# A three-layer transformer block on one core: softmax maxima and residual of the second attention moved to TensorE, and four steps reordered

## The reference, cut to what matters

```
x = x + attn_a(layernorm(x))     # 16 heads of 64, causal, over the 256 tokens of a batch
x = x + ffn(layernorm(x))        # routed slots
x = x + attn_b(layernorm(x))     # below
x = x + ffn(layernorm(x))

def attn_b(x, Wq, Wk, Wv, Wo, bo):            # N=16 batches, S=256 tokens, D=128
    q = (x @ Wq.T).reshape(N, S, 16, 8).transpose(0, 2, 1, 3)      # k and v likewise
    att = einsum('nqhd,nkhd->nhqk', q, k)                          # q, k: head; h: token
    att = softmax(att / sqrt(8), axis=3)
    out = einsum('nhqk,nkhd->nqhd', att, v).reshape(N, S, D)
    return out @ Wo.T + bo
```

## Time and profile before

| what | value |
|---|---|
| three runs | 996.13, 1005.44, 1005.65 us (median 1005.44) |
| the profiled execution's own time | 997.58 us |
| its span in the profile | 995.8 us |
| PE busy | 814.4 us, 82% |
| PEld busy | 619.3 us, 62% |
| DVE busy | 698.0 us, 70% |
| ACT busy | 462.7 us, 46% |
| POOL busy | 409.1 us, 41% |
| TensorE's granted clock, mean | 0.914 |

### The profile page before, as it was taken

One profiled execution on the slowest core, in us unless ns is written; L12 is line 12 of the kernel. 1 busy time (PEld: TensorE's weight loads), 2 busy tenths in 40 slices (PEclk: granted clock), 3 DMA queues, 4 the chain that ended last, 5 costly groups with the idle time before them and its releaser, 6 DMA issues.

```text
span 995.8 us, 25347 instructions
## 1 busy us (share of the span) xinstructions
PE 814.4 (82%) x10180; PEld 619.3 (62%) x10180; DVE 698.0 (70%) x1589; ACT 462.7 (46%) x785; POOL 409.1 (41%) x302
## 2 busy tenths in 40 slices
PE   2999999999999999999958766678777877829655
PEld 1688788887888888888845535345455445415435
DVE  4666666667666676666675775478989898867764
ACT  1667666667666676667632321222233233204220
POOL 1445444544444454444431000056767767751000
PEclk9999999999999999999988787778999999957776
DMA  6000000000000000000000000001111111110002
GB/s 258 2 3 1 0 0 0 0 0 0 0 0 0 0 0 0 0 0 0 2 1 1 1 1 1 1 3 19 21 11 21 21 14 18 22 21 1 1 1 84
DMA packets 71585, 13.16 MB, mean 13 GB/s; under 512 B 66432, under 2 KB 70528, under 8 KB 70912
## 3 DMA queue, kind: packets, MB, share of 16 engines
q1 hardware_dynamic: 71552, 12.71, 5.9%
HBM read 8.51 MB, written 4.19 MB: 13 GB/s over the span
## 4 chain that ended last, share of the span: by engine, by line
PE 56%; DVE 19%; issue 10%; ACT 10%; POOL 3%; DMA 1%; DVEq 0%; ACTq 0%; SPq 0%; POOLq 0%
PE PS L519 6%; PE PS L476 4%; PE PS L335 4%; PE PS L692 3%; PE PS L412 3%; DVE b_prod L776 3%; PE PS L337 3%; PE PS L483 3%; PE PS L336 3%; ACT a_ph L545 3%; PE PS L512 2%; PE PS L683 2%; PE PS L957 2%; PE PS L455 2%; POOL b_w L833 2%
## 5 line engine op out<-in xcount | busy, mean ns | idle before, releaser
L620 POOL TENSOR_TENSOR a_pl<-a_p,a_ph 128x1024 f16<-128x1024 f32 (+1 forms) x128 | 210.4, 1643 | 270.6 <-ACT a_ph L545 270.6
L542 ACT ACTIVATE a_p<-PS 128x1024 f32<-128x1024 f32 (+1 forms) x128 | 103.8, 811 | 89.1 <-PE PS L483 89.1
L833 POOL TENSOR_TENSOR b_w<-b_v,b_e 128x2048 f32<-128x2048 f32 x32 | 136.9, 4301 | 0.0
L587 DVE TENSOR_REDUCE a_nm<-PS 128x4 bf16<-128x512 f32 (+1 forms) x128 | 121.1, 946 | 0.4 <-PE PS L455 0.4
L576 DVE TENSOR_TENSOR a_qk_l<-PS,a_qk_h 128x512 f16<-128x512 f32 x128 | 87.9, 687 | 46.7 <-ACT a_qk_h L535 46.6
L545 ACT ACTIVATE a_ph<-PS 128x1024 f16<-128x1024 f32 (+1 forms) x128 | 102.9, 804 | 0.0
L535 ACT ACTIVATE a_qk_h<-PS 128x512 f16<-128x512 f32 x128 | 72.2, 604 | 58.0 <-PE PS L337 57.9
L683 PE MATMUL PS<-b_kh,w_rolls 128*128 128x256 f16 x256 | 68.7, 296 | 30.9 <-DVE b_prod L776 29.8
L776 DVE TENSOR_TENSOR b_prod<-PS,b_qt 128x512 f32<-128x512 f32 x128 | 84.1, 678 | 13.9 <-PE PS L685 13.7
L358 POOL TENSOR_TENSOR veps<-mv,eps 128x2 f32<-128x2 f32 (+2 forms) x40 | 7.9, 197 | 190.3 <-DVE mv L1107 139.1
L583 DVE TENSOR_TENSOR a_vl<-PS,a_vh 128x512 f16<-128x512 f32 x64 | 44.3, 692 | 54.8 <-ACT a_vh L538 54.8
(11 more groups left out here) (212 smaller groups left out, 2069.9 us busy)
## 6 DMA issues: line engine op xcount, KB each, us to landing
scratch_dram<-b_o SPq DMA_DIRECT2D x32, 64.0 KB, 4.0
b_y<-scratch_dram SPq DMA_DIRECT2D x16, 128.0 KB, 2.0
out_dram<-X SPq DMA_DIRECT2D x2, 1024.0 KB, 3.9
w_rest<-rest_dram SPq DMA_DIRECT2D x1, 1846.0 KB, 15.1
X<-x_dram SPq DMA_DIRECT2D x1, 1792.0 KB, 11.2
w_first<-first_dram SPq DMA_DIRECT2D x1, 1600.0 KB, 6.8
w_rolls<-rolls_dram SPq DMA_DIRECT2D x1, 512.0 KB, 15.3
X<-x_dram SPq DMA_DIRECT2D x1, 256.0 KB, 3.3
```

What stands on the lines that cost most here:

```text
L542: act.activation((a_p0, a_p1)[j][:, me, :, :, :].rearrange("p a h q -> p a (h q)"), TT[:, :, 0:512 - 256 * j], ACT.Exp, scale=EA ** -0.5)
L587: dve.tensor_reduce(a_nm[:, nx, j, :].rearrange("p (a h) -> p a h", a=2)[:, :, 0:2], MM[:, :, 0:256 * (j + 1)].rearrange("p a (h k) -> p a ...
L620: pool.tensor_tensor(*(n[:, g % 2, :, :, :].rearrange("p a h q -> p (a h q)") for n in (pl, p, ph)), ALU.subtract).then_inc(a_split, 1)
L833: pool.tensor_tensor(b_w8[:, j, :, :, :], rolled_values(par, j, 0, H), rolled_exps(par, j, 0, H), ALU.mult).then_inc(b_weighed, 1)
```

## The change

Eight things are changed.

- First attention: in each group `lo 0` comes behind `maxrow`; in group 2 `xt` comes behind `exps 1` and `exph 1`.
- Second attention, maxima: VectorE reduces them negated and rounded to bf16 (`b_nm`); a new step `shift` adds them on TensorE to the scores in the bank, by a product with the bf16 identity, and ScalarE takes the exponential straight from the bank. `flip` no longer starts the bank afresh with each product but with its first alone. `v` and the matmuls of roll 0 (`early`) are ahead of `soft`.
- Residual and bias: `project` first adds the bias in two f16 halves for both tiles at once, then `X` by a product with the identity, then Wo. `add` is now a copy by ScalarE.
- `normal` comes between `weigh 0` and `weigh 1`.
- `roll 7` comes ahead of `xt`.
- `qk`: ScalarE copies K first, then waits for K's low half, then copies Q and raises a new semaphore `b_q`, for which roll 0 on VectorE and the next fill of the bank wait.
- The last statistics wait for the added batches, since another engine writes them.
- Three small VectorE instructions are added to the constants.

```diff
@@ -74,8 +74,9 @@
             steps.extend((kind, g, n) for kind, n in new if cond)
-        put(prepare, ("qk", 0), ("qk", 1), ("lo", 0))
+        put(prepare, ("qk", 0), ("qk", 1))
         put(True, ("maxrow", 0))
+        put(prepare, ("lo", 0))
         put(not (first and g < 2), ("normal", 0))
...
         put(g == 2 and not last, ("apply", 0))
@@ -87,11 +88,11 @@
         put(g == 1 and not last, ("norm", 0))
-        put(g == 2 and not last, ("xt", 0))
         put(prepare, ("masks", 1))
...
         put(True, ("exps", 1), ("exph", 1))
+        put(g == 2 and not last, ("xt", 0))
         put(g == 1 and not first, ("project", 0))
...
         put(last and g == 3, ("ffn_apply", 0))
@@ -107,22 +108,26 @@
             steps.extend((n[0], par, n[1]) if isinstance(n, tuple) else (n, par, 0) for n in names)
+    put(one, "v", "early")
     put(True, "soft")
     put(two, "norm")
-    put(one, "v", ("roll", 0), ("roll", 1))
+    put(True, "shift")
+    put(one, ("roll", 0), ("roll", 1))
     put(before, "yt")
-    put(former, ("gather", 1), "normal")
+    put(former, ("gather", 1))
     put(two, "apply")
-    put(True, ("weigh", 0), ("weigh", 1))
+    put(True, ("weigh", 0))
+    put(former, "normal")
+    put(True, ("weigh", 1))
     put(one, ("roll", 2))
...
     put(before, "add")
-    put(one, ("roll", 6), ("flip", 0))
+    put(one, ("roll", 6), ("flip", 0), ("roll", 7))
     put(two, "xt")
-    put(one, ("roll", 7), ("dots", 1))
+    put(one, ("dots", 1))
     put(True, ("gather", 0))
...
     put(one, ("flip", 1))
@@ -133,7 +138,7 @@
               ("project", 1, 0)]
-B_PROLOGUE = [("norm", 0, 0), ("apply", 0, 0), ("xt", 0, 0), ("qk", 0, 0), ("v", 1, 0)]
+B_PROLOGUE = [("norm", 0, 0), ("apply", 0, 0), ("xt", 0, 0), ("qk", 0, 0), ("v", 1, 0), ("early", 1, 0)]
 for m in range(ROLLS):
...
 B_PROLOGUE += [("flip", 1, 0), ("flip", 1, 1), ("norm", 1, 0), ("apply", 1, 0), ("xt", 1, 0), ("qk", 1, 0)]
@@ -242,7 +247,8 @@
         ident, identb = w["ident"], w["identb"]
-        ones = sb("ones", [128, 128])
+        ones, ones_h = sb("ones", [128, 128]), sb("ones_h", [1, 128], F16)
+        b_bo_h, b_bo_l = sb("b_bo_h", [1, D], F16), sb("b_bo_l", [1, D], F16)
         a_wqk_h, a_wqk_l = sb("a_wqk_h", [128, 8, 2, 128], F16), sb("a_wqk_l", [128, 8, 2, 128], F16)
...
         b_w_h, b_w_l = sb("b_w_h", [128, 3, 128], F16), sb("b_w_l", [128, 3, 128], F16)
@@ -312,7 +318,7 @@
         b_e = sb("b_e", [128, 2, QT, H, H])
-        b_m, b_rs = sb("b_m", [128, QT, H]), sb("b_rs", [128, 2, QT, H])
+        b_nm, b_rs = sb("b_nm", [128, QT, H], BF16), sb("b_rs", [128, 2, QT, H])
         b_w8 = sb("b_w8", [128, QT, H, EB, H])
...
         b_o = sb("b_o", [128, QT, H, EB])
@@ -625,9 +631,10 @@
         b_stats, b_rstd, b_normed = sem("b_stats"), sem("b_rstd"), sem("b_normed")
+        b_q = sem("b_q")
         b_xh, b_xl, b_hi, b_lo, b_values = sem("b_xh"), sem("b_xl"), sem("b_hi"), sem("b_lo"), sem("b_values")
         b_rolled, b_multiplied, b_dotted = sem("b_rolled"), sem("b_multiplied"), sem("b_dotted")
-        b_shifted, b_exped, b_weighed, b_normal = sem("b_shifted"), sem("b_exped"), sem("b_weighed"), sem("b_normal")
+        b_maxed, b_shifted, b_exped, b_weighed, b_normal = sem("b_maxed"), sem("b_shifted"), sem("b_exped"), sem("b_weighed"), sem("b_normal")
         b_raised, b_flipped = sem("b_raised"), sem("b_flipped")
...
         b_stored, b_loaded, b_turned, b_added = sem("b_stored"), sem("b_loaded"), sem("b_turned"), sem("b_added")
@@ -645,7 +652,7 @@
             b = 2 * i + par
-            return {"qk": (b_lo, b + 3), "v": (b_values, b + 2), "yt": (b_turned, b - 1), "project": (b_added, b - 1),
+            return {"qk": (b_q, b + 3), "v": (b_values, b + 2), "yt": (b_turned, b - 1), "project": (b_added, b - 1),
                     "xt": (b_xl, b + 3)}[kind]
...
         def b_tensor(pe):
@@ -674,7 +681,12 @@
                     ins.then_inc(b_filled, 1)
-                elif kind == "roll":
+                elif kind == "shift":
+                    pe.wait_ge(b_maxed, b + 1)
+                    pe.matmul(O[par][:, :].rearrange("p (t s h) -> p t s h", t=QT, s=H), identb[:, :],
+                              b_nm[:, :, :].unsqueeze(2).to_broadcast([128, QT, H, H]), start=False, stop=True,
+                              skip_group_check=True).then_inc(b_shifted, 1)
+                elif kind == "early" or kind == "roll" and j > 0:
                     m = ROLLS * (b + 1) + j
...
                         pe.wait_ge(b_lo, b + 2)
@@ -695,14 +707,14 @@
                     if j == 0:
-                        wait(pe, b_shifted, b)
+                        wait(pe, b_exped, b)
                     for t in range(QT):
...
                                             ident[:, :].rearrange("p (n h) -> p n h", n=4)[:, :, 0:H],
-                                            start=True, stop=True)
+                                            start=j == 0 and t == 0 and e == 0, stop=False, skip_group_check=True)
                     ins.then_inc(b_flipped, 1)
...
                     pe.wait_ge(b_loaded, 16 * (b - 1))
@@ -711,14 +723,24 @@
                     pe.wait_ge(b_turned, b - 1)
+                    for bo in (b_bo_h, b_bo_l):
+                        pe.matmul(dst[:, 0:SEQ].rearrange("p (t d) -> p t d", t=QT), ones_h[:, :],
+                                  bo[:, :].unsqueeze(1).to_broadcast([1, QT, D]), start=bo is b_bo_h, stop=False,
+                                  skip_group_check=True)
                     for t in range(QT):
                         out_t = dst[:, t * 128:(t + 1) * 128]
-                        pe.matmul(out_t, b_yt[:, t * 128:(t + 1) * 128], w["b_wo"][:, :], start=True, stop=False)
-                        ins = pe.matmul(out_t, ones[0:1, :], w["b_bo"][:, :], start=False, stop=True)
+                        pe.matmul(out_t, ident[:, :], X[:, one_tile((b - 2) * QT + t), :].rearrange("p a d -> p (a d)"),
+                                  start=False, stop=False, skip_group_check=True)
+                    for t in range(QT):
+                        out_t = dst[:, t * 128:(t + 1) * 128]
+                        ins = pe.matmul(out_t, b_yt[:, t * 128:(t + 1) * 128], w["b_wo"][:, :], start=False,
+                                        stop=t == QT - 1, skip_group_check=True)
                     ins.then_inc(b_filled, 1)
...
         def b_scalar(act):
+            bank = [None]
+
             def do(step, i, fill):
...
                 b = 2 * i + par
@@ -728,8 +750,9 @@
                 elif kind == "qk":
-                    act.activation(b_qt[:, par, :], src[:, 0:SEQ], ACT.Copy)
                     act.activation(b_kh[:, par, :], src[:, SEQ:2 * SEQ], ACT.Copy).then_inc(b_hi, 1)
+                    act.wait_ge(b_lo, b + 3)
+                    act.activation(b_qt[:, par, :], src[:, 0:SEQ], ACT.Copy).then_inc(b_q, 1)
                 elif kind == "apply":
...
                     for t in range(QT):
@@ -745,20 +768,30 @@
                     act.activation(b_st[:, j, :], M[j][:, :], ACT.Copy).then_inc(b_raised, 1)
-                elif kind == "soft":
+                elif kind == "shift":
                     act.wait_ge(b_shifted, b + 1)
-                    act.activation(b_e[:, par, :, :, :], b_e[:, par, :, :, :], ACT.Exp, scale=EB ** -0.5).then_inc(b_exped, 1)
+                    act.activation(b_e[:, par, :, :, :], O[par][:, :].rearrange("p (t s h) -> p t h s", t=QT, s=H),
+                                   ACT.Exp, scale=EB ** -0.5).then_inc(b_exped, 1)
+                elif kind == "project":
+                    bank[0] = R[fill.bank], fill.count
+                elif kind == "add":
+                    projected, count = bank[0]
+                    act.wait_ge(b_filled, count)
+                    act.activation(X[:, bass.ds((b - 2) * QT, QT), :], projected[:, 0:SEQ]
+                                   .rearrange("p (t d) -> p t d", t=QT), ACT.Copy).then_inc(b_added, 1)
                 elif kind == "yt":
...
         def b_vector(dve, chain):
-            link, bank = chain.link, [None]
+            link = chain.link
 
...
                 if kind in ("ffn_stats", "ffn_apply"):
+                    if kind == "ffn_stats":
+                        dve.wait_ge(b_added, NB // 2)
                     early_norm(dve, link, kind, 1)
...
                     norm_stats(dve, link, X, (b + 2) * QT, QT).then_inc(b_stats, 1)
@@ -771,6 +804,8 @@
                     dve.wait_ge(b_rolled, ROLLS * (b + 1) + j + 1)
+                    if j == 0:
+                        dve.wait_ge(b_q, b + 2)
                     if j % 4 == 0:
...
                     dve.tensor_tensor(b_prod[:, j, :, :], T[j % 2][:, :].rearrange("p (e t) -> p e t", e=2),
@@ -779,9 +814,7 @@
                     sc = O[par][:, :].rearrange("p (t s h) -> p t h s", t=QT, s=H)
-                    link(dve.tensor_reduce(b_m[:, :, :], sc, X_AXIS, ALU.max))
```

(16 more changed lines are left out.)

## The result

The changed kernel takes 973.52 us (median of four runs, 972.47 to 975.52), the one before 1001.64 on the same footing (four runs, 996.13 to 1005.65): a ratio of 0.9725, 95% interval [0.9664, 0.9787]. The forecast was 980 from 1001, a ratio of 0.979. The kernel before runs at one of two levels: of 27 later executions 25 took 995.3 to 998.7 us and two about 1005, so the two at 1005 among the four here raise its median, and 23 to 25 us is a fairer size of the gain than 28. The profiled execution of the changed kernel took 972.47 us with a span of 970.7.

A forecast was written before the change was run, and what follows sets the result against it. TensorE was taken to bound the first attention, VectorE to pace the second. The terms, −2.0 − 17.5 − 1.2 − 0.6 + 0.4 = −20.9 us, taken off 1001, gave 980; range 966 to 998.

The forecast's parts named there:

- (a): First attention, `lo 0` behind `maxrow`: TensorE's gaps ahead of the maxima's product go, 0.65 us a batch, 10.4 us off.
- (b): First attention, `xt` behind `exph 1` in group 2: 0.89 us wait becomes about 1.7 elsewhere, costing 0.56 a batch, 8.4 us.
- (c): Second attention, maxima added on TensorE: VectorE loses the subtraction, 0.72 us a batch off the path.
- (d): Second attention, residual add moved to TensorE: frees 0.33 us of VectorE, costs TensorE 0.25 us a batch.
- (e): Second attention, roll 7 ahead of `xt`: 0.45 us less a batch, the chain then being roll 7, dots, projection, flip.
- (f): Second attention, `weigh 0` ahead of `normal`: hidden in steady state, 1.6 us off the last batch, 1.2 us net.
- (g): Second attention, `qk` copies K before Q: 0.6 us off in the two prologue batches, hidden in steady state.
- Rival 1: Second attention: the DRAM round trip is late, TensorE stands at `yt`, 0.5 to 0.6 us a batch back: 989; chance 0.12.
- Rival 3: First attention: the turning's new wait is covered, 8.4 us on become 13 off: 959; chance 0.04.
- Rival 4: Second attention: something unseen, such as TensorE's order, sets the pace and VectorE's freed time is idle: 999; chance 0.06.
- Rival 2: First attention gives nothing: the maxima's gap moves to the next wait, the turning costs 8.4 us: 990; chance 0.10.
- Rival 5: First attention: the turning's new 1.7 us wait lets TensorE's clock fall, 2 us lost a batch: 1010; chance 0.06.

The follow-up runs named there:

- experiment 3: Changed kernel with both edits of the first attention undone (`lo 0` ahead of `maxrow`, turning at its old place): 971.59 us, batch 30.55 us.
- experiment 1: Changed kernel with the turning of the next input (`xt`) in the first attention back at its old place: 962.45 us, batch 30.07 us.
- experiment 7: Changed kernel with the residual added by VectorE again, the bias still in two f16 products: 975.2 us.
- experiments 5 and 10: Changed kernel with roll 7 behind the turning again: 982.98 us; changed kernel with roll 7 and the turning both ahead of flip 0: 971.87 us.
- experiment 8: Changed kernel with maxima and their subtraction on VectorE again, `v` and roll 0 behind `soft`: 986.25 us.
- experiment 9: Kernel before the change with six unread f16 products more per batch of the second attention (batches 2 to 13): 993.32 us against 997.33.

## Why the prediction was right, point by point

The direction and the size were right: 20.9 us off the profiled run were forecast, 25.1 measured, 2.4 of which lie in a stage that the change doesn't touch. That the size came out so near is in part luck: the first attention missed by 6.0 us to the one side, and the clock, which the sum did not have, gave about 6 to the other.

- **(a) `lo 0` behind `maxrow`: half right.** All gaps ahead of the maxima's product closed, but the term was 0.65 us a batch and the edit is worth 0.48 (experiment 3 against 1). The step that failed is that `v` was the only consumer looked at. `pv` waits for the division, which is next in VectorE's order, and its first load comes 0.23 after the division's end. Counted from the start of the row's transpose, the division ends at 2.04 in all groups; before it was 2.13, 2.13, 1.75 and 2.04. "Copy and subtraction together end when they did" so held in groups 0, 1 and 3; there the division is no later, but in 1 and 3 TensorE arrives sooner and gets 0.16 and 0.08 of the 0.24 and 0.16 that were counted. In group 2, which had no gap, the division comes 0.29 later and `pv` 0.09; the turning's wait is 0.1 shorter for it. (The row of waits has 47 of them, not the 48 that the bound used.)
- **(b) the turning: right in its mechanism, under-sized.** A loss was forecast, 0.56 us a batch; it is 0.51 with `lo 0` in its old place and 0.77 beside edit (a). The projection started 0.57 after `xl`, not 0.48, and the third of (a)'s gaps was counted although (b) had already made room for it. So the first attention lost 4.0 us instead of gaining 2.0, within the bounds of (b), and experiment 1 takes 10 to 11 us back.
- **(c) maxima on TensorE: right.** 0.72 us forecast, 13.28 to 14.01 measured.
- **(d) residual: right in time, wrong in a cost.** It frees VectorE time in which VectorE waits for roll 7 (experiment 7: 13.28 with and without), so in the loop it is worth nothing, and not because ScalarE's copy were dearer (0.38 us against 0.41 for the add). TensorE, which was to pay 0.25 us a batch, saves as much (last section).
- **(e) roll 7: right**, 0.45 forecast with (d) (its own links give 0.40 to 0.45), 0.54 measured. The chain named as the new bound is the one that experiments 5 and 10 move.
- **(f) weighing: right.** Hidden in the loop and 1.5 us at the end (forecast 1.6). The rest of the last stretch's 2.4 us goes, one profile each, to the residual (0.5, experiment 7) and the maxima (0.4, experiment 8: 24.85 us instead of 24.46). The round trip through DRAM fitted.
- **(g), (h)** lie within what the neighbouring stretches vary by.
- **What the sum lacked: the clock.** I had it as a rival, but only as a fall in the first attention, which never came. It rose in the second. The five long intervals of before stood 4.5 us above 14.55 in all, after one stands 1.0 above; the last interval's fall cost 1.1 (14.33 against 13.20 in experiment 9); and the first interval shrank by 2.9 us at a clock of 1.00 instead of 0.73, where 1.2 was forecast. Some 6 of the 24.2 us are so the clock's, an estimate from these differences, and 18 are left beside the 17.5 forecast. With all intervals at the regular pace the change is 14.55 to 13.28, 1.27 against a forecast of 1.17.

Rivals 1, 3 and 4 fall by the same rows: no wait for the load (1), the turning's new wait is in full view (3), and VectorE's freed time in (c) counts (4). Rival 2 came true in part: some of the maxima's gap did move to the next wait, and the first attention ended 4.0 us later, between the 2.0 gained of the forecast and the rival's 8.4 lost. Rival 5 did not come: waits of 1.64 us in every batch, and the clock stayed at 0.99.

## What to carry to other kernels

When a step is moved out of a wait, write down the whole chain that ends in the wait and ask which link became shorter. Here the wait was the end of a chain over three engines: moving its last link cost 0.8 us a batch, moving its first won 0.6. And when an order is swapped on an engine, look at every consumer of what stands behind the two instructions, not only at theirs. Work taken off an engine counts only up to the next wait of that engine: of two pieces taken off VectorE in one batch, the 0.72 us counted in full and the 0.33 not at all.

## What the runs showed of the hardware that I had not expected

**TensorE's clock in the second attention fell less often when TensorE was given more to do.** In the profile before, stretches at 1.2 GHz came in every third interval (granted clock 0.72 from 727 to 733 us), after products that waited for VectorE. Adding products that nobody reads, 0.66 us of them to each batch, kept the granted clock at 1.00 over 110 us where it had been 0.95, and the kernel got 0.4% faster. In the changed kernels with 13.3 us batches the clock was 1.00 from the third interval on, in the one with 14.0 us batches 0.98. Whether it is the amount of work or how it lies in time was not separated. So an edit that shortens a batch in which TensorE is not the bound can gain twice.

**Bias products with one row were dearer than they looked.** Before, a batch's projection was two Wo products and two one-row f32 products in turns, 0.31 us from the first to the second and then 0.42 apart; it ran from 712.65 to the next roll at 714.21:

```profile
712.65 0.39 PE L716 MATMUL PS<-w_rest,b_yt 128*128 128x128 f32 x2
...
714.21 0.28 PE L683 MATMUL PS<-b_kh,w_rolls 128*128 128x256 f16 x1
```

After, with two f16 one-row products first and then four f32 products of 128 rows one behind the other, the whole takes 709.34 − 708.03 = 1.31 us instead of 1.56, though it does more:

```profile
708.03 0.28 PE L727 MATMUL PS<-b_bo_h,ones_h 1*128 1x256 f16 x1
708.15 0.27 PE L727 MATMUL PS<-b_bo_l,ones_h 1*128 1x256 f16 x1
708.35 0.71 PE L732 MATMUL PS<-X,w_first 128*128 x4
708.89 0.61 PE L736 MATMUL PS<-w_rest,b_yt 128*128 128x128 f32 x4
709.34 0.27 PE L695 MATMUL PS<-b_kh,w_rolls 128*128 128x256 f16 x1
```

The four f32 products are 0.25 us apart. In experiment 7's kernel, which has the same bias products and Wo products without those of `X`, the whole takes 0.87 us (707.00 to 707.87). So the new bias products save 0.69 us and the residual's cost 0.44; the forecast had counted 0.42 for each of the old bias products and as much for each of the residual's. Whether it is the turn between one row and 128 or the f32 product with one row that costs was not tried.
